# A two-layer graph network on one core: inverse root degrees by one-hot products instead of table gathers, and two passages of ScalarE's order moved

## The reference, cut to what matters

```
h  = relu(layernorm(x))                        # layer 0: attention-like messages
xn = layernorm(h) * ln_g + ln_b
q, k, v = xn @ Wq.T + bq, xn @ Wk.T + bk, xn @ Wv.T + bv
dk, dv  = silu(edge_attr @ Wdk.T + bdk), silu(edge_attr @ Wdv.T + bdv)
a   = silu(sum(q[dst] * k[src] * dk, 1)) * cosine_cutoff(edge_weight)
agg = segment_sum(v[src] * dv * a[:, None], dst)
x   = x + h + agg @ Wo.T + bo

h    = relu(layernorm(x))                      # layer 1: normalised graph convolution
deg  = segment_sum(edge_weight, src) + 1       # self-loops of weight 1
dinv = where(deg > 0, rsqrt(deg), 0)
h7   = segment_sum((h @ W)[dst] * (dinv[src] * edge_weight * dinv[dst])[:, None], src) + dinv**2 * (h @ W) + b
out  = x + relu(h7 @ W1 + b1) @ W2 + b2
```

## Time and profile before

| | us |
|---|---|
| median of 3 runs | 2006.33 |
| lowest, highest | 2002.97, 2006.59 |
| the profiled execution, its time | 2008.08 |
| the profiled execution, its span | 2006.4 |

### The profile page before, as it was taken

The page is one execution under the profiler, slowest core; times in us unless marked ns, Lnnn a source line. Parts: engine busy times, 40 slices in busy tenths (PEclk is TensorE's granted clock), DMA queues, the critical chain, the costliest instruction groups (busy, mean ns, idle before and its releaser), DMA issues.

```text
span 2006.4 us, 30280 instructions
## 1 busy us (share of the span) xinstructions
PE 1598.3 (80%) x6241; PEld 1047.8 (52%) x6241; DVE 1343.3 (67%) x5623; ACT 1188.1 (59%) x2271; POOL 1343.7 (67%) x996
## 2 busy tenths in 40 slices
PE   5917989898989898254445424999999999999999
PEld 2304555555555555133333313666767666666766
DVE  7945656665666664555455538788888888888883
ACT  5914555554555554122221226888989898989984
POOL 2044788888888885688888876566666666666660
PEclk9958999999999999666665656999999999999999
DMA  7995555555555556354454568899999999999981
GB/s 246 418 353 198 154 161 160 152 142 155 162 160 148 145 156 172 78 88 88 88 91 84 88 124 212 248 254 265 275 269 273 266 273 264 272 270 267 274 254 70
DMA packets 153340, 391.94 MB, mean 195 GB/s; under 512 B 24660, under 2 KB 68796, under 8 KB 153292
## 3 DMA queue, kind: packets, MB, share of 16 engines
q1 hardware_dynamic: 88844, 258.08, 38.1%
q0 software_dynamic: 59552, 115.52, 30.9%
q10 hardware_dynamic: 4896, 17.83, 2.3%
HBM read 211.36 MB, written 179.98 MB: 195 GB/s over the span
## 4 chain that ended last, share of the span: by engine, by line
PE 38%; DMA 18%; POOL 17%; issue 12%; ACT 7%; DVE 6%; ACTq 1%; SPq 1%; DVEq 0%; POOLq 0%
PE bank L1381 15%; PE bank L1370 15%; DMA sums_dram<-ub,sidx 7%; POOL cg L487 6%; DMA kept<-in_x_dram,look 5%; POOL sums_dram L483 5%; PE bank L1360 4%; PE bank L1221 3%; DMA cg<-sums_dram,ic 3%; ACT z L1068 2%; POOL kept L487 1%; DVE cg L875 1%; POOL tab_d L487 1%; DVE st L737 1%; POOL kept L569 1%
## 5 line engine op out<-in xcount | busy, mean ns | idle before, releaser
L483 POOL DMA_INDIRECT sums_dram<-ub,sidx x196 | 317.8, 1622 | 84.0 <-issue 43.5
L1370 PE MATMUL bank<-kept,w 128*128 128x512 f32 x784 | 355.8, 597 | 0.0
L569 POOL TENSOR_TENSOR kept<-kept 128x1024 f32<-128x1024 f32 x98 | 233.6, 2383 | 182.2 <-DVE cg L952 182.2
L1381 PE MATMUL bank<-w_sb,kept 128*128 128x256 f32 x1568 | 354.3, 379 | 0.0
L1381 PEld LDWEIGHTS bank<-w_sb,kept 128*128 128x128 f32 x1568 | 297.9, 190 | 81.9 <-issue 46.4
L1335 PE MATMUL bank<-cg,en 128*128 128x256 f32 x392 | 173.1, 619 | 204.7 <-ACT cg L1126 199.7
L1280 PE MATMUL bank<-qkv_w,zT 128*128 128x512 f32 x392 | 210.4, 662 | 80.6 <-ACT zT L1038 80.5
L1335 PEld LDWEIGHTS bank<-cg,en 128*128 128x128 f32 x392 | 117.8, 314 | 259.7 <-issue 235.2
L479 POOL TENSOR_TENSOR b_rs<-b_ve,minus_half 128x8 f32<-128x8 f32 x102 | 210.2, 2061 | 24.1 <-DVE b_ve L969 24.1
L1370 PEld LDWEIGHTS bank<-kept,w 128*128 128x128 f32 x784 | 142.8, 192 | 142.6 <-issue 142.5
L1147 ACT ACTIVATE kept<-kept,b_nb,b_rs 128x256 f32<-128x256 f32 x392 | 202.2, 589 | 16.6 <-DVE b_nb L942 16.6
(11 more groups left out here) (185 smaller groups left out, 3198.7 us busy)
## 6 DMA issues: line engine op xcount, KB each, us to landing
sums_dram<-cg SPq DMA_DIRECT2D x162, 512.0 KB, 13.3
kept<-in_x_dram SPq DMA_DIRECT2D x97, 512.0 KB, 5.5
kept<-sums_dram POOLq DMA_DIRECT2D x97, 512.0 KB, 9.9
cg<-sums_dram SPq DMA_DIRECT2D x97, 512.0 KB, 8.6
out_dram<-cg SPq DMA_DIRECT2D x97, 512.0 KB, 9.7
sums_dram<-cg ACTq DMA_DIRECT2D x34, 512.0 KB, 6.3
row_d<-in_dst_dram SPq DMA_DIRECT2D x48, 128.0 KB, 3.5
row_s<-in_src_dram SPq DMA_DIRECT2D x48, 128.0 KB, 3.3
```

The lines of the kernel that those rows point to most:

```text
L483: pool.indirect_dma_start(sums, bass.IndirectOffsetOnAxis(idx, 0), rows, None, bounds_check=last_row, compute_op=ALU.add).then_inc(done, 16)
L569: pool.tensor_tensor(X1[k.slot(8)], X[k.slot(4)], H[k.slot(2)], ALU.add).then_inc(g_xh, 1)
L1370: ins = pe.matmul(bank[:, 2 + m, :], w01[:, c, m * P:(m + 1) * P], hT[k.slot(2)][:, c * GN:(c + 1) * GN], start=(c == 0), stop=(c == KC - 1))
L1381: ins = pe.matmul(to, rT[k.slot(2)][:, c * GN + j * P:c * GN + (j + 1) * P], w2_sb[:, c, :], start=False, stop=(c == KC - 1), skip_group_c ...
```

## The change

One number for each edge, dinv[dst], is looked up by a product instead of a gather. The key's partition of each dst is stored to DRAM as a float list (keys, edge order). In step s of the second edge pass SP broadcasts 256 of them to all partitions (row_k). VectorE compares them with each partition's number: HT[p, e] is 1 where edge e's key has partition p. TensorE multiplies: HT (128 x 128 edges) times dinv (128 x 392) gives for every edge the table row of its partition. VectorE picks the column with scalar_tensor_tensor, (iota == ckey) * row, whose sum goes to found. norm of the pair is found * weight, made in the step instead of once before.

Beside it: the stored table, its gathers and tab_d go. The pass over pairs of GpSimd's `messages2` is written out in Python instead of a loop, with its order kept (gather, power, scatter), and takes its indices from node_i, so VectorE's copy ic goes. In ScalarE's `messages` turned(1) stands before scaled(0) (before: after it), and silu_d(1) stands before the four relus (before: after them). VectorE waits for all fills before the second pass, since the selection writes into CG[0].

```diff
-        table = nc.dram_tensor("table_dram", (P * COLS, 1), F32).ap()
+        keys = nc.dram_tensor("keys_dram", (EC * P,), F32).ap()
...
-        tab_d = sb("tab_d", [P, EC, 1])
-        ic = ring("ic_", 2, [P, 2], I32)
+        row_k = ring("row_k_", 2, [P, 2 * P])
+        HT = ring("ht_", 2, [P, 2 * P])
+        found = sb("found", [P, EC])
+        picked = [CG[0].rearrange("p a d -> p (a d)")[:, i * COLS:(i + 1) * COLS] for i in range(4)]
...
@@ SP
-            sp.wait_ge(s_tab_sb, 1)
-            sp.dma_start(table.rearrange("(p c) k -> p (c k)", p=P), dinv[:, :]).then_inc(s_table, 16)
+            sp.wait_ge(s_key, 1)
+            sp.dma_start(keys.rearrange("(c p) -> c p", p=P), e_keyf[:, :]).then_inc(s_keys, 16)
...
+                    if k.past(2):
+                        pass_on(sp, (n_ht, k.value(-1)))
+                    elif not k.past(1):
+                        sp.wait_ge(s_keys, 16)
+                    sp.dma_start(row_k[k.slot(2)][:, :],
+                                 keys[bass.ds(k.value(0, 2 * P), 2 * P)].rearrange("(a e) -> a e", a=1)
+                                 .broadcast_to([P, 2 * P])).then_inc(n_key[k.slot(2)], 16)
@@ GpSimd, messages
-                k = p - 1
-                if 0 <= k < EP:
-                    if k == 0:
-                        pool.wait_ge(s_table, 16)
-                    for i in (2 * k, 2 * k + 1):
-                        gather(tab_d[:, i, :], table, look[:, i, 2:3], last_entry, m_tab)
@@ GpSimd, messages2 (new text; before: the same order in a loop, with pass_on and ic)
+                p = s.off
+                if p < EP:
+                    if p >= 2:
+                        pool.wait_ge(n_x1, p - 1)
+                    for i in range(2):
+                        gather(C0[p % 2][:, i, :], sums0, node_i[:, 2 * p + i, 0:1], last_row, n_c0[p % 2])
...
+            for p in range(EP + 1):
+                messages2(Step(p))
@@ VectorE
+            link(dve.tensor_scalar(e_key[:, :], e_rows[:, 1, :].bitcast(I32), 2, P - 1, ALU.logical_shift_right,
+                                   ALU.bitwise_and))
+            dve.tensor_copy(e_keyf[:, :], e_key[:, :]).then_inc(s_key, 1)
+            link(dve.tensor_scalar(part_f[:, :], dump_f[:, 0:1], float(-N), None, ALU.add))
...
-            dve.wait_ge(m_tab, 16 * EC)
-            link(dve.tensor_tensor(norm[:, :], tab_d[:, :, 0], ew_f[:, :], ALU.mult))
...
+            dve.wait_ge(s_fill, 16 * (NG + 1))
+            dve.wait_ge(s_fill1, 16 * NG)
...
+                k = s
+                q = k.slot(2)
+                if k.within(EP):
+                    dve.wait_ge(n_key[q], k.turns(2))
+                    if k.past(2):
+                        dve.wait_ge(n_look, k.value(-1))
+                    dve.tensor_scalar(HT[q][:, :], row_k[q][:, :], part_f[:, 0:1], None, ALU.is_equal).then_inc(n_ht, 1)
                 a = s.back(1)
                 q = a.slot(2)
                 if a.within(EP):
+                    dve.wait_ge(n_look, a.value(1))
+                    for i in range(2):
+                        ins = dve.scalar_tensor_tensor(
+                            picked[2 * q + i], iota_c[:, :],
+                            ckey[:, bass.ds(a.value(0, 2) + i, 1), 0], bank[:, 2 + 2 * q + i, 0:COLS],
+                            ALU.is_equal, ALU.mult, accum_out=found[:, bass.ds(a.value(0, 2) + i, 1)])
+                    ins.then_inc(n_sel, 1)
                     dve.wait_ge(n_c0[q], a.turns(2, 32))
...
+                    dve.wait_ge(n_sel, a.value(1))
+                    dve.tensor_tensor(cols(norm, a), cols(found, a), cols(ew_f, a), ALU.mult).then_inc(n_norm, 1)
@@ ScalarE, messages
-                if s.back(3).within(EP):
-                    scaled(0)
                 if s.back(4).within(EP):
                     turned(1)
                 if s.back(3).within(EP):
+                    scaled(0)
                     scaled(1)
+                if s.back(4).within(EP):
+                    silu_d(1)
                 k = s.back(1)
...
-                if s.back(4).within(EP):
-                    silu_d(1)
@@ TensorE, messages2, ahead of U
+                k = s
+                q = k.slot(2)
+                if k.within(EP):
+                    if not k.past(1):
+                        for done, n in ((m_msg, EC), (m_at, EC), (m_ST, EP)):
+                            pe.wait_ge(done, n)
+                    pe.wait_ge(n_ht, k.value(1))
+                    if k.past(2):
+                        pe.wait_ge(n_sel, k.value(-1))
+                    for i in range(2):
+                        ins = pe.matmul(bank[:, 2 + 2 * q + i, 0:COLS], HT[q][:, i * P:(i + 1) * P], dinv[:, :],
+                                        start=True, stop=True)
+                    ins.then_inc(n_look, 1)
...
-                for done, n in ((m_at, EC), (m_ST, EP), (m_UB, EP), (m_zT, EC)):
+                for done, n in ((m_at, EC), (m_ST, EP), (m_UB, EP), (m_zT, EC), (n_sel, EP)):
```

More of the change, by code:

```diff
@@ L282, in build @@
         fst2 = ring("fst2_", 4, [P, 2])
-        n_ic, n_row, n_c0, n_sc = sem("n_ic"), sems("n_row", 2), sems("n_c0", 2), sem("n_sc")
-        (n_x1, n_st, n_mv, n_ve, n_rs, n_nb, n_h, n_eq, n_cnt, n_en, n_fst, n_idx, n_U, n_UB) = [
-            sem("n_" + n) for n in "x1 st mv ve rs nb h eq cnt en fst idx U UB".split()]
+        n_row, n_key, n_c0, n_sc = sems("n_row", 2), sems("n_key", 2), sems("n_c0", 2), sem("n_sc")
+        (n_x1, n_st, n_mv, n_ve, n_rs, n_nb, n_h, n_eq, n_cnt, n_en, n_fst, n_idx, n_U, n_UB, n_ht, n_look,
+         n_sel, n_norm) = [sem("n_" + n) for n in "x1 st mv ve rs nb h eq cnt en fst idx U UB ht look sel norm".split()]
         def part(width):
@@ L494, in gather_x @@
                 for k in (2 * p, 2 * p + 1):
-                    gather(XS[k % 4], x, look[:, k, 1:2], last_node, m_x[p % 2])
-                    gather(kept[:, k, :], x, look[:, k, 0:1], last_node, m_x[p % 2])
+                    gather(XS[k % 4], x, node_i[:, k, 1:2], last_node, m_x[p % 2])
+                    gather(kept[:, k, :], x, node_i[:, k, 0:1], last_node, m_x[p % 2])
             def messages(p):
@@ L534, in messages2 @@
             def messages2(s):
-                k = s
-                q = k.slot(2)
-                if k.within(EP):
-                    w = [(n_ic, k.value(1))]
-                    if k.past(2):
-                        w.append((n_x1, k.value(-1)))
-                    pass_on(pool, *w)
-                    for i in range(2):
-                        gather(C0[q][:, i, :], sums0, ic[q][:, i:i + 1], last_row, n_c0[q])
-                k = s.back(1)
-                if k.within(EP):
-                    inv_sqrt(ve[k.slot(2)][:, :, :], rs[k.slot(2)][:, :, :], n_ve, n_rs, k)
-                k = s.back(5)
-                if k.within(EP):
-                    w = [(n_UB, k.value(1)), (n_idx, k.value(1))]
-                    if k.past(1):
-                        w.append((n_sc, k.value(0, 32)))
-                    else:
-                        w.append((s_fill1, 16 * NG))
-                    pass_on(pool, *w)
+                p = s.off
+                if p < EP:
+                    if p >= 2:
+                        pool.wait_ge(n_x1, p - 1)
+                    for i in range(2):
+                        gather(C0[p % 2][:, i, :], sums0, node_i[:, 2 * p + i, 0:1], last_row, n_c0[p % 2])
+                k = p - 1
+                if 0 <= k < EP:
+                    inv_sqrt(ve[k % 2][:, :, :], rs[k % 2][:, :, :], n_ve, n_rs, s.back(1))
+                k = p - 5
+                if 0 <= k < EP:
+                    pool.wait_ge(n_UB, k + 1)
+                    pool.wait_ge(n_idx, k + 1)
+                    if k >= 1:
+                        pool.wait_ge(n_sc, 32 * k)
+                    else:
+                        pool.wait_ge(s_fill1, 16 * NG)
                     for i in range(2):
-                        scatter_add(sums1, sidx2[k.slot(4)][:, i:i + 1], UB[2 * k.slot(2) + i], n_sc)
-            run_steps(pool, EP, 1, 4, PAIR_STEPS + 3, messages2)
+                        scatter_add(sums1, sidx2[k % 4][:, i:i + 1], UB[2 * (k % 2) + i], n_sc)
+            for p in range(EP + 1):
+                messages2(Step(p))
             def nodes(s):
@@ L915, in messages2 @@
                                       ALU.add).then_inc(n_idx, 1)
-                k = s.back(-1)
-                if k.within(EP):
-                    if k.past(2):
-                        pass_on(dve, (n_c0[k.slot(2)], k.back(2).turns(2, 32)))
-                    ends(k)
             run_steps(dve, EP, 1, 4, PAIR_STEPS + 3, messages2)
```

20 lines of the change are left out of this document (9 added, 11 removed).

## The result

| | before | after |
|---|---|---|
| median of the runs of this comparison | 2004.65 us (4 runs, 2002.54 to 2006.59) | 1932.2 us (4 runs, 1929.72 to 1933.64) |
| the profiled execution, time and span | 2008.08, 2006.4 | 1933.64, 1932.0 |
| mean granted clock | 0.888 | 0.93 |
| dk/dv product of pair 3, of pair 45 | 193.68, 745.57 | 185.70, 647.05 |
| first gather of the second pass | 811.9 | 712.5 |

The ratio is 0.9637, with a 95% interval of 0.9621 to 0.9654: 72 us faster. The forecast was 1928 us. Behind the total stand two misses that nearly cancel: the first pass brought 15 us more than forecast, and the second pass lost 28.5 us where 5 were forecast. Both periods of the second pass are taken here between the power of pair 8 and that of pair 43.

What follows compares the result with a forecast made beforehand. GpSimd was taken to bound both edge passes and TensorE the node pass. 2008.1 - 75 (first pass) - 8 (start) + 5 (second pass) = 1930, brought to the median 1928 us; likeliest range 1910 to 1950, with rivals 1900 to 1980.

Steps and rivals of the forecast that it cites:

- The first pass, -75: First edge pass: without table gathers TensorE bounds it, 13.14 to 11.35 us a pair, gain 75 us, bounds 111 and 35.
- Rival 1: First pass: late landing of gathers moves into TensorE's chain, period near 12.3 us, time 1968 us, chance 0.15.
- rival 2: First pass: the reorder does more and the period follows GpSimd, 10.6 us, time about 1896 us, chance 0.05.
- The start, -8: Start of first pass: x gathers go some 14 us earlier, partly lost to full DMA and ScalarE's fills; 8 us taken.
- The drain, 0: End of the first pass: the same chain of pairs and scatters, so no change, 0.
- The second pass, +5: Second edge pass: GpSimd stays the bound, added work hidden but for 0.1 us a pair; +5 us, bounds -3 and +25.
- hidden by that lead: Second pass, SP: the added broadcast of 256 keys, issued two pairs ahead, costs nothing.
- GpSimd waiting for ub: Second pass: a wait of GpSimd for ub as a sign that the forecast is wrong, put to the rivals there; no size.
- rivals 3 and 4: Second pass: selections cost 2.6 us, time 2050, chance 0.04; the lookup's wait lengthens TensorE's loop, time about 1987, chance 0.09.
- GpSimd beside VectorE, 0.1 us a pair: Second pass: HT falls on GpSimd's scatter and slows it by 0.1 us a pair, 5 us; 20 us by the skill's rule.
- The node pass, 0: Node pass: bound by TensorE, its code untouched, the bank opening's wait already satisfied; no change, 0.
- The last sign: Node pass: a start less than 60 us earlier than 1162 would show the forecast wrong.

Runs made afterwards that it cites:

- e_no_gathers: The kernel before without the two table gathers of a pair and nothing in their place, dinv[dst] left out of the weights: 1920.5 us.
- e_timed_ring: The changed kernel with the sources' broadcast waiting for the scatter's landing, and four key buffers instead of two, loaded two pairs earlier: 1909.2 us.
- e_order_alone: The kernel before with ScalarE's new order of the first pass alone: 1998.7 us, ratio 0.9974.
- e_load_added: The kernel before with one more 128 KB broadcast a pair in the second pass, waited for but never computed with: 2093.3 us.
- the timed ones: Changed kernels whose sources' broadcast waits for the scatter's landing: 1921.0 us with two key buffers, 1909.2 with four, 1907.4 with keys loaded ahead.

## Why the prediction was right, and where it was wrong

- **The first pass, -75.** Right in mechanism: GpSimd is no longer the bound, TensorE is. That the gathers were nearly all of it, and the reorder about 0.2 us a pair, is in e_no_gathers. The size was off: 10.98 and not 11.35 us a pair, 42 x 2.155 = 90.5 us, and just under the 11.0 to 11.8 to which the chance of 0.62 was given. The 11.36 us of the drain were the old order's, with its short waits on the copy zT in them; undone, the order gives 11.17 to 11.26. Rival 1 (12.3) and rival 2 (10.6) did not come.
- **The start, -8.** 193.68 became 185.70: -8.0. The x gathers of pair 2 leave GpSimd at 109.73, 17 us earlier, and VectorE's statistics of them come 16.7 us earlier (137.63 became the row below). As forecast, not all of it came through. Of the two reasons given, the one that the rows show is ScalarE's stores: z and zT stand behind them, 10.21 and 9.09 us with nothing else to wait for (ACTq: issued by ScalarE).

```profile
120.92 0.75 DVE L739 BATCH_NORM_STATS2 st<-cg 128x6 f32<-128x256 f32 x2 [5.83 <-DMA kept<-in_x_dram,node_i]
...
130.88 2.07 ACT L1080 ACTIVATE z<-cg,nbz,rs 128x255 f32<-128x255 f32 x4 [10.21 <-issue]
...
134.80 9.02 ACTq L1043 DMA_DIRECT2D sums_dram<-cg  x6
143.86 0.60 ACT L1050 ACTIVATE zT<-bank 128x512 f32<-128x512 f32 x1 [9.09 <-issue]
```

- **The drain, 0.** 66.3 us from the product of pair 45 to the first gather of the second pass before, 65.45 after.
- **The second pass, +5.** This is the step that failed: the stretch from its first gather to the node pass went from 410.2 to 439.6 us; with the 0.9 of the drain that is 28.5 us lost, just outside the +25 that I allowed. The failing sentence is that SyncE's extra broadcast is "hidden by that lead". It is, for the one who reads it. It is not for the scatters: SyncE is released by VectorE's eq at a moment that falls on the second scatter, and the pass had a loop through that scatter's landing with hardly any slack (7.38 of 7.43 us) that I had not looked for. I read GpSimd's rows, saw no wait, and took GpSimd for the only bound. The trace had the sign: in the earlier trace rows the scatter at 1008.82 stands behind a gap of 0.50 us, not of 0.30, and ub had started at 1007.97, 0.85 us before it. The prediction's own sign of being wrong, GpSimd waiting for ub, did come, but it had been put to rivals 3 and 4, and the cause is neither.
- **The rest of the second pass.** Selections 0.62 us (0.6 taken), HT 0.36 (0.4), the lookup's product by the rows 1.58 us for four at the high clock and 2.98 at the low one (1.45 and 2.9). Rivals 3 and 4 did not come: TensorE waits for HT, but nobody waits for the lookup. One reading of the rows was loose: the four k/v instructions at 434.94 take 2.79 us, which is neither the low level (3.78 for four) nor the high one (1.97 at 406.24), so they ran partly at each. The price at the low level does not rest on them.
- **GpSimd beside VectorE, 0.1 us a pair.** None: 7.38 us a pair with HT, selections and products (e_timed_ring), 7.38 without them (e_no_gathers). In 26 pairs of e_timed_ring (from 800 to 1110 us) HT, 0.40 us long, is under way when a scatter's issue starts, and each of these takes 1.63 to 1.65 us, as any other. Single scatters did take up to 2.12 us in place of 1.6: in the 8 of e_timed_ring that took over 1.75 from 780 to 1110 us, it is VectorE's x1 (L894, 0.69 us, an addition of two SBUF tiles, there before the change too) that is under way at the start, and the scatter is the longer the more of x1 is left (in two more pairs x1 starts 0.03 us ahead, takes 0.75 us itself, and the scatter its usual time). The Trainium skill, "SBUF — State Buffer", Who interferes with whom, would allow a block for the whole of HT if it runs in a two-port mode; no run shows in which mode it runs, and none shows a block by it.
- **The node pass, 0.** It became 4.4 us shorter. In the kernel before VectorE stands once for 5.91 us at its second round of steps there, with nothing released:

```profile
1297.38 0.16 DVE L939 TENSOR_TENSOR b_rs<-b_rs,dinv 128x4 f32<-128x4 f32 x1 [5.91 <-issue]
```

  TensorE then waits 3.95 us, and its clock falls to 0.66 for 10 us. The stall is there in e_order_alone (6.0 us), e_load_added (5.7) and e_no_gathers (5.4), whose VectorE programs are nearly that of before, and in none of the changed kernel and the nine others made from it, which all have the longer one. What the engine does in it was not tested.

- **The signs.** The period of the second pass was to be 7.4 to 7.6 us, and is 8.06. The last sign, "a node pass that starts less than 60 us earlier than 1162", is miswritten. Read as a node pass that starts after 1162, it did not come: it starts at 1152.1, 70 us earlier than before.

So the span's sum reads: 98.5 us ahead at pair 45, of which 8 from the start, less 28.5, plus 4.4, is 74.4; the forecast's own sum was 78. That the two are so close is luck: the gains of the first pass (15.5 us), the drain and the node pass (5.3) that were not forecast and the loss of the second pass that was not (24.4) nearly cancel.

## What to carry to other kernels

In this kernel an added transfer was hidden from its reader and not from another transfer. So before calling one hidden, ask two parties: whoever reads its data, and whoever waits for another transfer that is in flight at the same time. Look for a loop of the kind "issue, landing, next issue", compare its length with the engine's own work, and see at which point of the loop the new transfer is released; where it falls on the last link, an extra wait that issues it right behind the landing was worth more here (1921.0 us, and 1909.2 with deeper buffers) than half the bytes (1925.7). And where a bracket blames an instruction that itself waits for a DMA, check in the code whether both wait for the same event.

## What the runs showed of the hardware

- Two scatter-adds of 128 KB each, seen from the issue of the second to the instruction that waits for both: 3.8 to 4.0 us with no broadcast issued in between (the pairs 42 and 43 of nearly every kernel, and all pairs of the timed ones), 4.5 to 4.8 in the mean with one of 128 KB, 4.94 with one of 128 and one of 64 KB, 5.1 to 5.4 with two of 128 KB, and 6.7 in e_load_added, with two of 128 KB as well. The bytes alone do not give the size. That the transfers meet at all, though one comes from SyncE and the other from GpSimd, is what the Trainium skill says ("DMA: Bandwidth & Descriptors", Issuing engines are not separate DMA queues); it gives no size. In the timed kernels the same broadcasts fall beside the gap and the first scatter, and cost nothing that the period shows.
- The first scatter of a pair starts 0.83 to 0.86 us after ScalarE's ub, which waits for the same landing, where nothing else holds it.
- An indirect DMA's issue on GpSimd takes up to 0.5 us longer when VectorE's addition of two SBUF tiles (0.69 us) has just started; a compare of 128 x 256 (0.40 us) at the same place changes nothing (e_timed_ring).
- The same first-pass code ran between 10.98 and 11.13 us a pair in eight builds.
